# Gates six heads ahead, written into the result; bias tables from turned host tables; another order of products in a head step

## The reference, cut to what matters

```
qg, k, v = split(x @ w_qkv.T);  q, gate = split(qg)
q, k = layernorm(q) * w + b, layernorm(k) * w + b      # per head
q, k = rope(q), rope(k)                                # cos, sin tables
attn = softmax(causal(q @ k.T / sqrt(D)))
out = (attn @ v) * sigmoid(gate)
return out @ w_o.T
```

## Time and profile before

| | us |
|---|---|
| three runs | 929.83, 925.27, 930.14 (median 929.83) |
| profiled execution | 920.18, of it span 918.4 |
| PE busy | 747.6 (81%) |
| DVE / ACT / POOL busy | 543.4 / 310.5 / 253.9 |
| mean granted TensorE clock | 0.911 |

### The profile page before, as it was taken

How to read it: one execution, slowest core, us unless ns; L and a number is a source line. 1 busy time by engine, 2 the same in 40 slices (tenths; PEclk the granted TensorE clock), 3 DMA queues, 4 the chain that set the end, 5 groups by cost and what they waited for, 6 DMA issues and landing times.

```text
span 918.4 us, 13063 instructions
## 1 busy us (share of the span) xinstructions
PE 747.6 (81%) x4496; PEld 449.5 (49%) x4498; DVE 543.4 (59%) x1446; ACT 310.5 (34%) x809; POOL 253.9 (28%) x263
## 2 busy tenths in 40 slices
PE   4679999999999999999985497248999987937960
PEld 2345555566556655677843244224455535423530
DVE  5767777777777777331178174464555424944643
ACT  2345555555555555330031140011455442302200
POOL 1533333333333333000033605751100000343174
PEclk9989999999999999999997589766999978966995
DMA  7000000100000000001970322300000001012243
GB/s 268 0 1 35 1 1 24 34 0 0 23 0 0 0 23 1 1 1 70 374 265 1 92 70 87 97 23 1 2 1 1 1 2 47 0 46 76 80 121 93
DMA packets 18385, 45.09 MB, mean 49 GB/s; under 512 B 4256, under 2 KB 12832, under 8 KB 17952
## 3 DMA queue, kind: packets, MB, share of 16 engines
q1 hardware_dynamic: 13440, 31.20, 9.2%
q0 software_dynamic: 4896, 13.24, 4.9%
HBM read 36.76 MB, written 7.34 MB: 48 GB/s over the span
## 4 chain that ended last, share of the span: by engine, by line
PE 40%; DVE 31%; issue 11%; POOL 7%; ACT 5%; DMA 3%; another core or an unknown queue 2%; DVEq 0%; POOLq 0%; ACTq 0%
PE ps L1113 6%; PE ps L1134 5%; PE ps L1224 5%; POOL xg L508 4%; PE ps L1261 4%; DVE prod L989 3%; DVE probs L831 3%; DVE mb L763 3%; DVE hst L777 2%; DVE b_qk L888 2%; PE ps L1507 2%; PE ps L1334 2%; PE ps L1522 2%; DVE qT L786 2%
## 5 line engine op out<-in xcount | busy, mean ns | idle before, releaser
L817 DVE TENSOR_REDUCE negmax<-ps 128x1 f32<-128x512 f32 (+3 forms) x128 | 56.9, 485 | 92.5 <-PE ps L1137 92.5
L1099 PE MATMUL ps<-w_qkv_a,xnT 128*128 (+2 forms) x256 | 95.1, 499 | 5.8 <-ACT nq L543 5.1
L573 ACT COPY pT<-ps 128x512 f32<-128x512 f32 (+1 forms) x96 | 43.2, 523 | 136.3 <-PE ps L1211 136.3
L508 POOL DMA_INDIRECT xg<-y_rows,slot_of x64 | 65.6, 1025 | 84.8 <-DMA y_rows<-turn 66.1
L1134 PE MATMUL ps<-kT,qT 128*128 128x512 f32 (+3 forms) x256 | 86.6, 461 | 1.0 <-DVE kT L788 1.0
L452 POOL TENSOR_TENSOR hrs<-hve,half 128x5 f32<-128x5 f32 x32 | 38.5, 1203 | 175.9 <-DVE hneg L803 175.7
L543 ACT ACTIVATE nq<-ps,hnm,hrs 128x128 f32<-128x128 f32 x160 | 59.4, 459 | 62.8 <-POOL hnm L454 62.8
L888 DVE TENSOR_REDUCE b_qk<-ps 128x2 f32<-128x1024 f32 (+1 forms) x64 | 49.8, 820 | 46.3 <-PE ps L1266 46.3
L1149 PE MATMUL ps<-pT,vA 128*128 128x512 f32 (+3 forms) x256 | 75.9, 440 | 0.0
L1224 PE MATMUL ps<-xnT,w_gate 128*128 128x512 f32 x128 | 63.0, 614 | 9.7 <-DVE kT L788 8.5
L434 POOL TENSOR_TENSOR ln_rs<-ln_ve,half 128x4 f32<-128x4 f32 x8 | 8.7, 1081 | 224.6 <-DVE ln_ve L695 224.6
(11 more groups left out here) (162 smaller groups left out, 1381.3 us busy)
## 6 DMA issues: line engine op xcount, KB each, us to landing
w_down<-in_w_down SPq DMA_DIRECT2D x1, 4096.0 KB, 14.2
y_rows<-turn SPq DMA_DIRECT2D x32, 128.0 KB, 1.7
w_qkv_a<-in_w_qkv SPq DMA_DIRECT2D x4, 768.0 KB, 5.6
w_gate<-in_w_gate SPq DMA_DIRECT2D x4, 512.0 KB, 3.4
w_o<-in_w_o SPq DMA_DIRECT2D x1, 2048.0 KB, 13.5
xn_rows<-xn SPq DMA_DIRECT2D x2, 1024.0 KB, 9.7
x_res<-in_x SPq DMA_DIRECT2D x2, 512.0 KB, 4.1
xg<-y_rows,slot_of POOLq DMA_INDIRECT x64
```

What stands on the lines that cost most here:

```text
L508: pool.indirect_dma_start(out=gath[:, n % 2, j], out_offset=None, in_=y_dram, in_offset=bass.IndirectOffsetOnAxis(ap=slot_of[:, j, n:n + 1 ...
L817: op = dve.tensor_reduce(negmax[:, kp, i4:i4 + 1], wide[:, at:at + (i4 + 1) * P], AX, ALU.max, negate=True)
L1099: mm = pe.matmul(dst, xnT[:, k, col:col + P], w, start=(k == 0), stop=(k == KT - 1))
```

## The change

- PE projects the gate of head k + 6 in head k's step, behind the key projection and ahead of the turn of the five heads. The gates of heads 0 to 5 are projected in steps 0 to 3, in banks 2, 3 and 6 (GATES_IN); the last six head steps have none. Bank 2 holds gates alone; the turned keys go to bank 7, which the values' product uses, so the turn waits for oT and the values' product for kT.
- ACT's tanh writes straight into oT, at the end of its step, and DVE multiplies oT in place. The buffer `gate` is gone.
- The order within the ten transposes is by bank, with a count for each of the three banks. ACT's three copies to pT stand at the head of its next step, each behind its own count. PE goes from the transposes to the next scores.
- ACT's copy of the values moves ahead of the exponentials; every fourth step it waits for the values' product of this step, in the others for the one before. DVE takes the key moments ahead of turned(), and copies kT ahead of qT.
- The host gives turned cos and sin tables (cosT, sinT, 256 KB each), the norm weights with a half-swapped copy (nvec), and the biases as columns (nbias). ACT scales sinT (swapT) and DVE makes biasT with one instruction for each of two tables; rotA and rotB take one each for two tables too, without the steps for a turned bias. PE turns no tables.
- Loads: first half of x, ident, first query weights, nvec and tables, second half of x, gate weights, and so on. The second half of x is normalised in steps 0 and 1, and turned by PE at the end of step 0.

```diff
@@ -347,13 +356,15 @@
-        TURN_AT = (0, 4, 4, 4)
+        XN_BANKS = ((0, 1, 6, 7),) + 3 * ((4, 5, 6, 7),)
+        GATES_IN = {0: ((0, 2), (1, 3)), 1: ((2, 2), (3, 6)), 2: ((4, 2),), 3: ((5, 6),)}
...
@@ -372,25 +383,26 @@
         @block.sync
         def _(sp):
             sp.dma_start(x[:, 0:ST, :], t["x"][0].rearrange("(n p) d -> p n d", p=P)).then_inc(ld_x[0], 16)
-            sp.dma_start(x[:, ST:NT, :], t["x"][1].rearrange("(n p) d -> p n d", p=P)).then_inc(ld_x[1], 16)
-            sp.dma_start(ident[:], t["ident"]).then_inc(ld_const, 16)
+            sp.dma_start(ident[:], t["ident"]).then_inc(ld_id, 16)
+            sp.dma_start(wq[:, 0], t["w_qkv"][0]).then_inc(ld_wq[0], 16)
+            sp.dma_start(nvec[:], t["nvec"]).then_inc(ld_const, 16)
             sp.dma_start(cosf[:], t["cosf"]).then_inc(ld_const, 16)
             sp.dma_start(sinf[:], t["sinf"]).then_inc(ld_const, 16)
-            sp.dma_start(nvec[:], t["nvec"]).then_inc(ld_const, 16)
-            sp.dma_start(identb[:], t["identb"]).then_inc(ld_const, 16)
-            sp.dma_start(maskb[:], t["maskb"]).then_inc(ld_const, 16)
-            for g in range(KV):
-                if g >= 2:
-                    sp.wait_ge(kv_mm, 8 * (g - 1))
+            sp.dma_start(x[:, ST:NT, :], t["x"][1].rearrange("(n p) d -> p n d", p=P)).then_inc(ld_x[1], 16)
+            sp.dma_start(wg[:], t["w_gate"][0]).then_inc(ld_wg, 16)
+            sp.dma_start(nbias[:], t["nbias"]).then_inc(ld_turn, 16)
+            sp.dma_start(cosT[:], t["cosT"]).then_inc(ld_turn, 16)
+            sp.dma_start(sinT[:], t["sinT"]).then_inc(ld_turn, 16)
+            sp.dma_start(identb[:], t["identb"]).then_inc(ld_mask, 16)
+            sp.dma_start(maskb[:], t["maskb"]).then_inc(ld_mask, 16)
+            sp.dma_start(wq[:, 1], t["w_qkv"][1]).then_inc(ld_wq[1], 16)
+            sp.dma_start(wo[:], t["w_o"]).then_inc(ld_wo, 16)
+            for g in range(2, KV):
+                sp.wait_ge(gate_mm, 8 * (g - 1))
+                sp.dma_start(wg[:], t["w_gate"][g - 1]).then_inc(ld_wg, 16)
+                sp.wait_ge(kv_mm, 8 * (g - 1))
                 sp.dma_start(wq[:, g % 2], t["w_qkv"][g]).then_inc(ld_wq[g % 2], 16)
-                if g >= 2:
-                    sp.wait_ge(gate_mm, 8 * (g - 1))
-                if g != 1:
-                    sp.dma_start(wg[:], t["w_gate"][max(g - 1, 0)]).then_inc(ld_wg, 16)
-                if g == 1:
-                    sp.dma_start(wo[:], t["w_o"]).then_inc(ld_wo, 16)
             sp.wait_ge(gate_mm, 8 * (KV - 1))
             sp.dma_start(wg[:], t["w_gate"][KV - 1]).then_inc(ld_wg, 16)
...
-                                   ps[:, TURN_AT[r] + c, :].rearrange("p (n k q) -> p n k q", n=2, k=KT)).then_inc(xnT_ready, 1)
-            xnT_copies(0)
+                                   ps[:, XN_BANKS[r][c], :].rearrange("p (n k q) -> p n k q", n=2, k=KT)).then_inc(xnT_ready, 1)
+            def open_gate(k, bank, i=None):
+                g, h, st = group_of(k, i), k % REP, (k // REP) % 2
+                dst = oT[:, g * REP + h, st] if i is None else oT[:, ds(g * REP + h, 1), st].rearrange("p a b -> p (a b)")
+                nc.scalar.activation(dst, ps[:, bank, :], ACT.Tanh, scale=0.5).then_inc(gate_done, 1)
+            xnT_copies(0, range(2))
+            act.wait_ge(scaled, 1)
             for c in range(2):
-                act.wait_ge(tab_turned, c + 1)
-                nc.scalar.copy(biasT[:, c], ps[:, 4 + c, :]).then_inc(tab_ready, 1)
+                nc.scalar.activation(swapT[:, c], sinT[:], ACT.Identity, scale=nbias[:, 2 * c + 1:2 * c + 2]).then_inc(swap_part, 1)
             def step(s, r, i=None):
+                if r == 1:
+                    xnT_copies(0, range(2, 4))
+                if LAG < r < LAST:
+                    act.wait_ge(p_turned, (s - LAG) * 3 - 2)
+                    nc.scalar.copy(pT[:, 0:S], wide[:, 0:S]).then_inc(pT_done, 1)
+                    act.wait_ge(p_turned, (s - LAG) * 3 - 1)
+                    nc.scalar.copy(pT[:, S:2 * S], wide[:, S:2 * S]).then_inc(pT_done, 1)
+                    act.wait_ge(p_turned, (s - LAG) * 3)
+                    nc.scalar.copy(pT[:, 2 * S:WIDE], wide[:, 2 * S:WIDE]).then_inc(pT_done, 1)
                 if 1 <= r <= TILES:
                     act.wait_ge(head_rs, s)
...
@@ -542,16 +570,18 @@
...
-                if r >= LAG + 1:
-                    act.wait_ge(gate_mm, s - LAG)
-                    if r >= LAG + 3:
-                        act.wait_ge(oT_done, s - LAG - 2)
-                    nc.scalar.activation(gate[:, (r - LAG - 1) % 2], ps[:, 2, :], ACT.Tanh, scale=0.5).then_inc(gate_done, 1)
+                    act.wait_ge(kv_mm, s)
+                    if r >= LAG + 1:
+                        act.wait_ge(pv_mm, s - LAG if (r - 1) % ST == 0 else s - LAG - 1)
+                    nc.scalar.copy(vA[:, ((r - 1) // ST) % 2, (r - 1) % ST],
+                                   ps[:, first_bank(r - 1) + 1, KC:2 * KC]).then_inc(v_done, 1)
+                for k, bank in GATES_IN.get(r, ()):
+                    act.wait_ge(gate_mm, k + 1)
+                    open_gate(k, bank)
                 if LAG <= r < LAST - 1:
                     kp = (r - LAG) % 2
                     if r >= LAG + 1:
-                        act.wait_ge(p_turned, s - LAG)
+                        act.wait_ge(p_turned, (s - LAG) * 3)
...
-                if 1 <= r <= TILES:
-                    act.wait_ge(kv_mm, s)
-                    if r >= LAG + 1:
-                        act.wait_ge(pv_mm, s - LAG)
-                    nc.scalar.copy(vA[:, ((r - 1) // ST) % 2, (r - 1) % ST],
-                                   ps[:, first_bank(r - 1) + 1, KC:2 * KC]).then_inc(v_done, 1)
-                if LAG <= r < LAST - 1:
-                    act.wait_ge(p_turned, s - LAG + 1)
-                    for a, b in ((0, S), (S, 2 * S), (2 * S, WIDE)):
-                        nc.scalar.copy(pT[:, a:b], wide[:, a:b]).then_inc(pT_done, 1)
+                if LAG <= r < LAG + HEADS - LEAD:
+                    act.wait_ge(gate_mm, s + (LEAD - LAG + 1))
+                    open_gate(r - LAG + LEAD, 2, i)
...
-            for b in range(B):
-                ln_apply(0, b)
-            dve.wait_ge(ld_const, 6 * 16)
-            dve.tensor_scalar(nvec[:, 0:2], nvec[:, 0:2], HD ** -0.5, None, ALU.mult).then_inc(tab_step, 1)
-            dve.wait_ge(tab_step, 1)
...
-            for c in range(2):
-                w, b = nvec[:, 2 * c], nvec[:, 2 * c + 1]
-                dve.tensor_tensor(halves(rotA[:, c]), halves(cosf[:]), over_tiles(w), ALU.mult).then_inc(tab_step, 1)
-                dve.tensor_tensor(halves(rotB[:, c]), halves(sinf[:]), over_tiles(w, True), ALU.mult).then_inc(tab_step, 1)
-                if c == 1:
-                    dve.wait_ge(tab_turned, 1)
-                ta, tb = [gate[:, n].rearrange("p (n d) -> p n d", d=HD) for n in range(2)]
-                dve.tensor_tensor(halves(ta), halves(cosf[:]), over_tiles(b), ALU.mult).then_inc(tab_step, 1)
-                dve.tensor_tensor(halves(tb), halves(sinf[:]), over_tiles(b, True), ALU.mult).then_inc(tab_step, 1)
...
+            ln_first(0)
+            ln_apply(0, 0)
+            dve.wait_ge(ld_const, 3 * 16)
+            for c, scale in enumerate((HD ** -0.5, 1.0)):
+                for k, (table, into) in enumerate(((cosf, rotA), (sinf, rotB))):
+                    dve.scalar_tensor_tensor(out=into[:, c], in0=table[:], scalar=scale,
+                                             in1=nvec[:, 2 * c + k:2 * c + k + 1].broadcast_to([P, ST, HD]), op0=ALU.mult,
+                                             op1=ALU.mult).then_inc(tab_made, 1)
+            dve.wait_ge(ld_turn, 3 * 16)
+            dve.tensor_scalar(nbias[:, 0:2], nbias[:, 0:2], HD ** -0.5, None, ALU.mult).then_inc(scaled, 1)
...
@@ -805,6 +822,11 @@
                 if r < LAG:
                     query_moments()
                     key_moments()
+                    if r == 0:
+                        ln_first(1)
+                    if r == 1:
+                        ln_apply(0, 1)
+                        bias_tables()
                     if r >= 1:
                         rotated()
                         turned()
...
+                    dve.scalar_tensor_tensor(out=dst, in0=dst, scalar=1.0, in1=ps[:, 7, :], op0=ALU.add,
                                              op1=ALU.mult).then_inc(oT_done, 1)
...
@@ -1114,6 +1128,16 @@
                                    wo[:, h], start=(h == 0), stop=(h == H - 1))
                 mm.then_inc(wo_mm, 1)
+            def project_gate(k, bank, i=None):
+                g, h, st = group_of(k, i), k % REP, (k // REP) % 2
+                if k % 8 == 0:
+                    pe.wait_ge(ld_wg, 16 * (g + 1))
+                for c in range(KT):
+                    mm = pe.matmul(ps[:, bank, :], wg[:, c, h * HD:(h + 1) * HD], xnT[:, c, st * S:(st + 1) * S],
+                                   start=(c == 0), stop=(c == KT - 1))
```

(51 more changed lines are left out.)

91 lines of the change are left out of this document (49 added, 42 removed).

## The result

| | us |
|---|---|
| before, median of 20 runs | 926.33 (922.98 to 933.43) |
| changed, median of 20 runs | 919.39 (911.09 to 927.77) |
| ratio changed to before | 0.990, 95% interval 0.9875 to 0.993 |
| predicted | 916 (907 to 925) |
| profiled execution changed | 922.67, span 920.8, granted clock 0.895 |

The same kernel was measured twice more, as e0_again and e8_after_again: ratios 0.994 (0.991 to 0.997) and 0.992 (0.989 to 0.995). The change gains between 0.6 and 1%; the forecast was 1.4%.

A forecast was written before the change was run, and what follows sets the result against it. PE plus a 0.6 us kT wait bound middle steps, a serial ACT and POOL loop the opening. 8.4 + 8.6 − 2.0 − 1.7 = 13.3 us off 920.18 gave 906.9, scaled by 1.05% to 916; range 907 to 925.

The forecast's parts named there:

- opening, to the first scores: Before the first attention scores: six gates added, tables' chain lost; scores at 53.5 instead of 51.81, cost 1.7 us.
- steps of heads 0 to 25, fourth steps in them: Middle of the first attention: 0.33 us saved in each of 26 steps, 8.6, less 2.0 for six fourth steps.
- last step with a projection of queries: Step before 357.76, queries but no gate: ends at 9.75 of 11.31 us, 1.5 saved.
- step of 357.76: Tail step without projections: heads' turn waits for oT until 7.8 us in; 9.7 instead of 10.51, 0.8 saved.
- the steps behind it, to the end: Tail from 368.27: no gate products; 1.5 us saved in one step, 4.6 in three with an output projection.
- The wait for kT: Middle steps: PE's 0.6 us hole between transposes and gate, waiting for DVE's kT, goes.
- the hole before the scores: After the transposes: PE waits 0.18 us for ACT's pT copy plus 0.1 to fill the pipe; new period 10.98.
- The turn's cover: Middle steps: oT is ready 7.8 us in, PE reaches the heads' turn at 9.07, so the wait is hidden by 1.3.
- The values' copy makes every fourth step late by 0.33: Every fourth middle step: exponentials queue behind the copy, oT at 9.4 against 9.07 us; six times, 2.0 lost.
- the lower clock: Rival for the opening: stops of about 2 us halve PE's speed afterwards; about +14 us, so 930; chance 0.05.
- The opening's own sign of being wrong: Check on the opening: the prediction is wrong if it ends after 58 us; scores were expected at 53 to 54.
- rule on transposes: Middle steps: transposes don't count as busy, so a block of 15, 1.6 us, would weigh towards the lower clock; given no effect.

The follow-up runs named there:

- e8_after_again: The changed kernel once more, nothing edited, beside the kernel before; 919.86 us against 925.41, ratio 0.992.
- e3_one_count: Changed kernel, but ACT waits for all ten transposes before the first of its three copies to pT; 942.0 us, ratio 1.017 to the kernel before.
- e2_values_late: Changed kernel, but in every fourth step ACT copies the values behind the exponentials; 914.76 us, ratio 0.9885 to the kernel before.
- e1_tanh_later: Changed kernel, but in the opening ACT opens each step's gates one step later; 916.7 us, ratio 0.991 to the kernel before.
- e5_filler: Changed kernel, with ten products nobody reads filling PE's stops in the opening and the last projecting step; 884.5 us, ratio 0.987 to the kernel before.
- e10_all_filled: Changed kernel, fourth-step values' copy behind exponentials; in the opening heads turned before gates, later tanh after step 0; nine unread products; 901.8 us, ratio 0.976 to before.

## Why the prediction was right, and what in it was off

The time fell into the range, on the side forecast; of the 13.3 us about half came (6.0 in the trace, 6.9 in the medians). That 919.39 lies so near to 916 is in part luck: the forecast was scaled from 929.83, the median of three runs, and the kernel before measured 926.33 over 20; from there the same 13.3 us would have given 913. By its own steps, in the trace:

| term | forecast | measured |
|---|---|---|
| opening, to the first scores | +1.7 | +5.9 |
| steps of heads 0 to 25, fourth steps in them | −6.6 | −5.7 |
| last step with a projection of queries | −1.5 | −1.35 |
| step of 357.76 | −0.8 | +1.2 |
| the steps behind it, to the end | −6.1 | −6.0 |
| sum | −13.3 | −6.0 |

- *The wait for kT goes; the hole before the scores is 0.18 and a pipe's 0.1.* Right to a hundredth: 10.98 forecast, 10.98 measured. That bank counts make it, and not luck, is shown by e3_one_count. The turn's cover was thinner than forecast: 0.7 us (oT at 8.43, PE at 9.16) and not 1.3.
- *The values' copy makes every fourth step late by 0.33.* The place is right (e2_values_late), the size was half: 0.65. The sum had oT end 9.4 us after the scores begin, the trace has 9.64 (110.04 + 0.68 less 101.08), most of it between the values' copy and the reciprocal, and PE starts the turn a further 0.15 later. The first head's step, 1.2 us shorter and counted at the common 0.33, made up for half of it.
- *The opening costs 1.7.* This is the step that failed; it cost 5.9. Its structure was right: ACT's order charges each gate, and e1_tanh_later, which moves only that, brings the scores back to 51.71. But the walk gave every projection 2.6 us, by rows at full speed, and put the lower clock down as a rival with 0.05, because stops of 2.1 us had not cost it. Of the 4.2 us that are missing, the slow third and fourth projections are 3.4 (nq 10.4 and 8.7 us apart in place of 8.7 and 7.0), and 0.5 lie before the first nq (23.88 for 23.4), where the first two tiles took 8.40 in place of 7.9. With the stops filled (e5_filler) the scores begin at 53.25, where the sum had 53.5, so it is the clock that was missing from it. The stops of 2.5 and 1.9 us were followed by the lower clock in all three profiles of this kernel, for 1.7 us each, once 2.6; a stop of 1.98 us before the fifth tile's projection never was, nor were those of the kernel before. What tells them apart these runs don't settle. The rival's price (+14) was too high: it held in two of three tiles and in no whole gate. The opening's own sign of being wrong, an end after 58 us, was missed by 0.3 us in the first profile and met in e8_after_again (58.18).
- *The step of 357.76 gets 0.8 shorter.* It got 1.2 longer: the turn started 8.58 us after the scores and not 7.8 (0.8; oT is out at 8.43 in this step as in every ordinary one, behind POOL and DVE's sum mb), and the longer stop of PE, 3.55 us with nothing to project, cost the clock in the 15 transposes behind it (1.2 by e5_filler). The prediction took the gates out of the tail and didn't ask what PE's clock does in the gap that they leave.
- *The gates' move out of the tail's last steps.* Right: 7.4 and 13.0 forecast, 7.39 and 13.04 measured.
- The Trainium skill's rule on transposes ("TensorE: Matmul & The Clock Gate", Part 4), weighed against the trace in the prediction, did nothing here: clock 1.00 in all ordinary middle steps with 15 transposes in a block. Part 1 of the same page of the Trainium skill has activity release the higher clock. e5_filler and e10_all_filled agree with that, with 4.5 against 2.85 us for a projection; the stop of 1.98 us that cost nothing shows that the length of a stop isn't the whole of it.

## What to carry to other kernels

Work moved from a busy stretch into one in which the engine stands isn't always free: here it stood in another engine's list (ACT's nq behind the gates' tanh), and it left a gap where it came from. Follow, for each moved product, which in-order list its consumer stands in, and prefer to let that consumer come one step late. Where a moved wait has cover of less than a microsecond, give buffers up piece by piece: three counts in place of one were worth 20 us. And where TensorE would stand for about two microseconds, as it did here, look at the granted clock behind the stop and price what follows at both of its levels.
